# First attention of a two-layer network: the scores below the 32nd pushed down before the exponential, by ScalarE and GpSimd, instead of a masked product on VectorE

## The chip, the cores and the metric

One core of one Trainium2 chip runs the whole network as one program. The metric is the device time of an execution in microseconds. The engines are TensorE (PE), VectorE (DVE), ScalarE (ACT), GpSimd (POOL) and SyncE (SP); each takes its instructions in order, and they wait for one another by semaphores.

## The reference, cut to what matters

The network has four parts on x of 16 batches by 256 rows by 128: a first cross-attention with a convolution and a feed-forward part, a small mixture of experts, a second cross-attention over all 1601 context rows, and a second mixture. Only the scores of the first are concerned. Each of its 4 heads has 256 query rows a batch and 1601 keys:

```
scores = einsum('bthd,bghd->bhtg', Q, K) / sqrt(DH)
topv, topi = top_k(scores, 32)
probs = softmax(topv)
attn = zeros_like(scores).at[..., topi].set(probs)
attn_mean = attn.mean(axis=1)          # over the heads
c_t = einsum('btg,bgd->btd', attn_mean, V)
```

So of a row's 1601 scores the 32 largest go through a softmax, all others become zero, and the four heads are averaged.

## The kernel before, in words

`attention0_phase` (from L417) works in **slots**. A slot is 128 query rows of one head of one batch: 2 tiles of rows by 4 heads make 8 slots (NS) a batch, 128 slots in all. `j` is the slot's number over all batches, `s` that within its batch. Batch 0 and batch 15 are written out, the 14 between run in a loop of two batches each (`walk`, L516). The order of the work is written out by hand: every engine has a `step(b, ...)` that goes over s from 0 to 7, and what it does beside the slot hangs on s. A slot goes like this:

- TensorE, `scores_of` (L682): the slot's scores, 128 x 1601, into four banks of PSUM; there is one such buffer. It is issued two slots ahead.
- ScalarE, `scores_out_of` (L813): copies them to `sc` in SBUF (four buffers), also two slots ahead.
- VectorE, `pieces_of` (L934): the eight largest of each of 32 pieces of 51 scores, one slot ahead. These 32 small maxima are put two at a time between the links of the next chain, so that its latencies are covered (`link`, inside `step`).
- VectorE: four times the eight largest of the 256 candidates (L966), each followed by a replacement of those found (L972). After the first, `negm` (minus the row's maximum, L968) is given to ScalarE. The last value is the 32nd largest, unless a piece held more than eight of the 32. Three reductions and a comparison (L974 to L978) tell whether that may be so, a **doubt**: the largest candidate left, or the eighth of any piece, is not under the threshold.
- ScalarE, `exp_of` (L820): exp of all 1601 scores into `pr` (one buffer for each s).
- VectorE, L986: the masked product. `pr` is multiplied by (score >= threshold).
- TensorE, `count_doubts` (L723): adds the doubts of the 128 rows by a product with a column of ones, into one number in PSUM. It is the first thing of TensorE's step.
- VectorE, `settle` (L924): converts the number of the slot before to an integer in SBUF (L927), loads it into a register and branches. If it is over zero, `select_all` (L912) finds the 32 largest again from all 1601 scores: four long maxima (L917), four replacements (L918) and a product (L919). Then it gives `top_ready` and `pr_ready`. That stands just before the masked product.
- ScalarE, `denominator` (L826): exp of the 32 values with their sum. VectorE, `weight` (L903): its reciprocal, times the row mask / 4. GpSimd, `make_diag` (L578): a diagonal matrix of it.
- TensorE, `transpose_probs` (L693): for the four heads of a tile, pr times the diagonal, added up in PSUM: that transposes, scales and averages at once. 13 key blocks go in four groups through two PSUM tiles (`tps`). GROUPS says which groups fall at which s: {1: (0,), 2: (1, 2), 3: (3,)}; the same at s + 4 for the other tile. Then `times_ctx` (L711) multiplies with the context.

Beside the slots, TensorE and ScalarE prepare the next batch and the later parts through one PSUM tile `misc`: a product, then ScalarE's copy, then the next product. There are 17 such jobs a batch: the film product (s = 0 and 4; `film`, L718 and L850), queries (s = 0), keys (s = 1, 2), transposed context (s = 4, 5), values (s = 6, 7). ScalarE's copies of them stand behind the slot's exponential and scores copy in its queue. GpSimd splits the keys into three bf16 parts (`split_keys`, L598, all at s = 3: three casts, two subtractions of 1601 columns), applies the film (L588), and SyncE stores the parts.

The next stage is `conv_phase` (from L996).

## Time and profile before

| | us |
|---|---|
| median of 3 runs (4032.58 to 4047.92) | 4040.31 |
| the profiled execution | 4040.28 |
| its span | 4038.7 |

| engine | busy us | share of the span |
|---|---|---|
| TensorE, products | 2940.5 | 73% |
| TensorE, weight loads | 1659.7 | 41% |
| VectorE | 2832.6 | 70% |
| ScalarE | 1684.6 | 42% |
| GpSimd | 550.0 | 14% |

A time in the span is in microseconds from its start. The first attention lies from about 193 to about 1846 us. A row of the profile names the engine, the line of the code, the operation, what is written and read, and how often; after a bar the busy time, the mean of one in ns, and the idle time of the engine just before it with what ended it. Matmuls overlap, so their durations add up to a little more than the time they take. PEclk is the granted TensorE clock as a share of 2.4 GHz.

### The profile page before, as it was taken

The numbers are of one execution on the slowest core, as the hardware profiler recorded it, in microseconds if no ns is written. First come the engines' busy times: TensorE is split into PE (matmuls) and PEld (weight loads), VectorE is DVE, ScalarE is ACT, GpSimd is POOL, SyncE is SP. The second block draws the span as 40 slices with busy tenths as digits, with TensorE's granted clock in tenths as the row PEclk, the third lists the DMA queues.
The fourth block names the chain that finished last, engine by engine and source line by source line (L and its number), as shares of the span: only waits on it lengthen the run. The fifth ranks groups of instructions, "written<-read, shape, count | busy, mean of one in ns | idle before, by whom it ended". The sixth has DMA issues, their size and how long they took to land. (4 is left out here: it accounts for less than half of the span.)

```text
span 4038.7 us, 71774 instructions
## 1 busy us (share of the span) xinstructions
PE 2940.5 (73%) x21156; PEld 1659.7 (41%) x21156; DVE 2832.6 (70%) x9302; ACT 1684.6 (42%) x2879; POOL 550.0 (14%) x721
## 2 busy tenths in 40 slices
PE   0047876878867787878965552489899899899748
PEld 0025554545544555657943220033333333333335
DVE  5578878888888887880055564988888888888212
ACT  1124433434433444431011001077777777778612
POOL 1011221212211222220011001200000000000133
PEclk9868888888888888886577665589999999999869
DMA  1000100100000010002301000522222222222121
GB/s 44 17 8 29 36 30 24 35 24 34 31 24 26 34 35 30 30 24 95 125 3 52 0 0 31 83 46 58 63 55 58 62 56 58 62 55 41 44 67 49
DMA packets 134711, 169.79 MB, mean 42 GB/s; under 512 B 50962, under 2 KB 103887, under 8 KB 134331
## 3 DMA queue, kind: packets, MB, share of 16 engines
q1 hardware_dynamic: 129694, 154.76, 13.9%
q0 software_dynamic: 4640, 10.76, 0.8%
q8 instruction: 144, 2.36, 0.2%
q14 instruction: 233, 1.91, 0.2%
HBM read 112.39 MB, written 53.51 MB: 41 GB/s over the span
## 5 line engine op out<-in xcount | busy, mean ns | idle before, releaser
L1919 DVE TENSOR_REDUCE mx<-wps 128x2 f32<-128x802 f32 x1024 | 957.9, 989 | 153.2 <-PE wps L1812 136.6
L1893 ACT ACTIVATE pb<-sps 128x512 f32<-128x512 f32 (+1 forms) x1664 | 896.6, 596 | 375.0 <-PE sps L1837 361.2
L937 DVE MAX8 cand<-sc 128x8 f32<-128x51 f32 (+1 forms) x4096 | 587.8, 198 | 34.8 <-ACT sc L818 34.6
L1850 PE MATMUL ops<-pb,va 128*32 128x256 f32 x6656 | 554.0, 406 | 7.6 <-ACT ot L1899 7.1
L690 PE MATMUL scores<-ctxT,qT 97*128 97x512 f32 (+1 forms) x1024 | 482.5, 624 | 6.3 <-ACT sc L818 3.2
L1812 PE MATMUL wps<-ks,qs 56*128 56x401 bf16 x2048 | 384.8, 361 | 109.0 <-DVE mx L1919 57.6
L706 PE MATMUL tps<-diag,pr 128*128 128x128 f32 (+1 forms) x3328 | 418.6, 288 | 5.7 <-issue 5.5
L1837 PE MATMUL sps<-qs,ks 59*128 59x256 bf16 (+1 forms) x3328 | 364.6, 284 | 63.6 <-DMA qs<-guards 63.1
L706 PEld LDWEIGHTS tps<-diag,pr 128*128 128x128 f32 (+1 forms) x3328 | 404.3, 200 | 8.3 <-issue 7.9
L986 DVE SCALAR_TENSOR_TENSOR pr<-sc,top,pr 128x1601 f32<-128x1601 f32 x128 | 251.4, 1964 | 151.4 <-issue 147.3
L690 PEld LDWEIGHTS scores<-ctxT,qT 97*128 97x128 f32 x1024 | 221.4, 228 | 254.7 <-issue 245.4
L824 ACT ACTIVATE pr<-sc,negm 128x1601 f32<-128x1601 f32 x128 | 208.5, 1629 | 225.9 <-DVEq L969 225.4
L1837 PEld LDWEIGHTS sps<-qs,ks 59*128 59x128 bf16 (+1 forms) x3328 | 120.7, 96 | 404.7 <-ACT pb L1893 242.5
L586 POOL TENSOR_SCALAR diag<-ident,rden 128x128 f32<-128x128 f32 x128 | 90.3, 705 | 1141.2 <-DVEq L910 937.1
L818 ACT COPY sc<-scores 128x1601 f32<-128x1601 f32 x128 | 190.5, 1488 | 79.8 <-PE scores L690 79.5
L1850 PEld LDWEIGHTS ops<-pb,va 128*32 128x32 f32 x6656 | 133.4, 110 | 213.1 <-issue 107.1
L1812 PEld LDWEIGHTS wps<-ks,qs 56*128 56x128 bf16 x2048 | 110.9, 97 | 244.4 <-DVE mx L1919 170.5
L1724 POOL COPY va<-vn 128x128 f32<-128x128 f32 (+1 forms) x208 | 50.3, 294 | 1095.8 <-PE ops L1850 1017.4
L840 ACT COPY prT<-tps 128x512 f32<-128x512 f32 (+1 forms) x128 | 64.6, 505 | 256.6 <-PE tps L706 256.6
L966 DVE MAX8 top<-cleft 128x8 f32<-128x256 f32 x384 | 157.2, 409 | 0.1
L972 DVE MATCH_REPLACE8 cleft<-top,cleft 128x256 f32<-128x256 f32 x384 | 157.1, 409 | 0.0
L728 PE MATMUL dps<-onecol,doubt 128*1 128x1 f32 x256 | 24.2, 163 | 175.4 <-DVEq L932 174.3
(370 smaller groups left out, 3610.4 us busy)
## 6 DMA issues: line engine op xcount, KB each, us to landing
ks<-keys SPq DMA_DIRECT2D x896, 50.0 KB
keys<-kpart SPq DMA_DIRECT2D x48, 400.2 KB, 2.8
toep<-kernpad SPq DMA_DIRECT2D x8, 2048.0 KB, 8.1
qs<-queries SPq DMA_DIRECT2D x896, 8.0 KB
values<-vs SPq DMA_DIRECT2D x16, 832.0 KB, 3.4
vn<-values SPq DMA_DIRECT2D x16, 832.0 KB, 4.8
ctxn<-in_ctx_dram SPq DMA_DIRECT2D x16, 576.0 KB
sorted<-m_blank SPq DMA_DIRECT2D x39, 130.0 KB, 3.2
```

The source lines that it names most:

```text
L690: ins = t.matmul(scores[:, c:c + n], q, ctxT[par][0:C + 1, c:c + n], start=True, stop=True)
L706: ins = t.matmul(tps[g % 2][0:kn(kt), (kt % 4) * P:(kt % 4) * P + P], pr[s0 + h][:, kt * P:kt * P + kn(kt)], diag[s0 + h][:, :], start=(h ...
L818: s_.copy(sc[s % 4][:, :], scores[:, 0:NK]).then_inc(scores_out, 1)
L824: s_.activation(pr[s][:, :], sc[s % 4][:, :], ACT.Exp, bias=negm[:, s:s + 1]).then_inc(exp_done, 1)
L937: st.add(v.max(cand[s % 2][:, n, :], sc[s % 4][:, c:c + w]))
L966: link(v.max(tp[:, 8 * r:8 * r + 8], x))
L986: st.link(v.scalar_tensor_tensor(out=pr[s][:, :], in0=sc[s % 4][:, :], scalar=tp[:, TOPK - 1:TOPK], in1=pr[s][:, :], op0=ALU.is_ge, op1=AL ...
L1812: ins = t.matmul(buf[:, 512 * odd:512 * odd + WIN], qs[par][r, h + odd, q * P:q * P + P], ks[par][r, h // 2, (WIN - 1) * c:(WIN - 1) * c + ...
L1837: ins = t.matmul(sps[(UNITS * g + u) % SB][0:kn(kt), i, :], ks[par][r, h // 2, kt * P:kt * P + kn(kt)], qs[par][r, h, :], start=True, stop ...
L1850: ins = t.matmul(ops[VW * i:VW * i + VW, 0:S], va[par][0:kn(kt), kt, 4 * g + i, :], pb[(UNITS * g + 2 * kt + i % 2) % 8][0:kn(kt), i // 2, :],
L1893: nc.scalar.activation(pb[(UNITS * g + u) % 8][0:rows_, :, :], sps[(UNITS * g + u) % SB][0:rows_, :, :], ACT.Exp).then_inc(p_ready, 1)
L1919: v.tensor_reduce(mx4[:, q, h:h + 2, c], both, AX.X, ALU.max).then_inc(work_read, 1)
```

## The change

The masked product goes. Instead, scores below the threshold are pushed far down before the exponential, so that it gives zero for them:

- GpSimd, `cut_of(s)`: waits for the threshold (`thr_ready`), clips it to +-2^46, multiplies it by 2^80 (`cutoff`), and makes `negm`. Three operations on one column.
- ScalarE, `below_of(s)`, one step later: relu(2^80 * (threshold - score)) into `pr`: zero for kept scores, huge for the others.
- GpSimd, `keep_of(s)`, in that same later step: `pr` = score - `pr`, over 128 x 1601.
- ScalarE, `exp_of(s)`, two steps later: exp of `pr` in place. It waits for `settled` and `kept_ready`.

The doubts are found by counting: one comparison over the 256 candidates and one over the 32 eighths, each with its sum, give for a row the candidates not under the threshold plus the pieces whose eighth is not; the branch asks whether the sum over the rows exceeds 128 x 32. ScalarE (`doubts_of`) copies the number from PSUM to SBUF as an integer, where VectorE did. VectorE's last replacement goes, `negm` and the product with the row mask go to GpSimd. `settle` and `weight` stand at the end of VectorE's slot. `select_all` now makes `pr` itself: a copy, eight long operations, a comparison and a sum. The transposes move one slot later (GROUPS), `split_keys` is spread over s = 3 to 7, the masks' constant is 2^45 in place of 1e30, and GpSimd clears this stage's semaphores at the end of its part of `conv_phase`.

```diff
 BIG = 1e30
+HIDDEN = 2.0 ** 45
 GONE = -3e38
...
             st.link(v.tensor_copy(mf[:, :], m8[:, :]))
-            v.tensor_scalar(mf[:, :], mf[:, :], BIG, -BIG, ALU.mult, ALU.add).then_inc(mask_done, 1)
+            v.tensor_scalar(mf[:, :], mf[:, :], HIDDEN, -HIDDEN, ALU.mult, ALU.add).then_inc(mask_done, 1)
...
+        k.used = []
+
         def sem(name):
-            return ctx.enter_context(nc.semaphore(name))
+            k.used.append(ctx.enter_context(nc.semaphore(name)))
+            return k.used[-1]
...
         cleft = sb("cleft", [P, len(PIECES), 8])
-        rest = sb("rest", [P, 2])
+        count = sb("count", [P, 2])
         doubt = sb("doubt", [P, 2])
-        doubts = sb("doubts", [1, 1], mybir.dt.int32)
+        doubts = sb("doubts", [1, 2], I32)
+        cut, cutoff = sb("cut", [P, NS]), sb("cutoff", [P, NS])
         onecol = sb("onecol", [P, 1])
...
         misc_ready, misc_out = sem("misc_ready"), sem("misc_out")
-        negm_ready, exp_done, top_ready, den_done, pr_ready = (sem("negm_ready"), sem("exp_done"), sem("top_ready"),
-                                                               sem("den_done"), sem("pr_ready"))
+        thr_ready, cut_ready, below_ready, kept_ready = sem("thr_ready"), sem("cut_ready"), sem("below_ready"), sem("kept_ready")
+        settled, exp_done, den_done = sem("settled"), sem("exp_done"), sem("den_done")
         rden_ready, diag_ready = sem("rden_ready"), sem("diag_ready")
...
                                                            sem("kparts_saved"), sem("vs_saved"))
-        doubt_ready, doubts_ready, general_step = sem("doubt_ready"), sem("doubts_ready"), sem("general_step")
+        doubt_ready, doubts_ready, doubts_out, general_step = (sem("doubt_ready"), sem("doubts_ready"), sem("doubts_out"),
+                                                               sem("general_step"))
         slot_begun, pool_passed = sem("slot_begun"), sem("pool_passed")
...
         HALVES = ((0, 1), (2, 3))
-        GROUPS = {1: (0,), 2: (1, 2), 3: (3,)}
+        GROUPS = {2: (0, 1), 3: (2, 3)}
+
+
+        STEEP, LIMIT = 2.0 ** 80, 2.0 ** 46
...
                 pool.sem_inc(pool_passed, 1)
+                st.link(g.tensor_tensor(rden[:, s:s + 1], rden[:, s:s + 1], k.tmask[:, bass.ds(QT * b + s // H0, 1)],
+                                        ALU.mult))
                 g.tensor_scalar(diag[s][:, :], ident[:, :], rden[:, s:s + 1], None, ALU.mult).then_inc(diag_ready, 1)
+
+            def cut_of(s, j):
+
+                pool.wait_ge(thr_ready, j + 1)
+                pool.sem_inc(pool_passed, 1)
+                c = cut[:, s:s + 1]
+                st.link(g.tensor_scalar(c, top[:, s % 4, TOPK - 1:TOPK], LIMIT, -LIMIT, ALU.min, ALU.max))
+                st.add(g.tensor_scalar(cutoff[:, s:s + 1], c, STEEP, 0.0, ALU.mult, ALU.add))
+                st.link(g.tensor_scalar(negm[:, s:s + 1], top[:, s % 4, 0:1], -1.0, 0.0, ALU.mult, ALU.add))
+                pool.sem_inc(cut_ready, 1)
+
+            def keep_of(s, j):
+
+                pool.wait_ge(below_ready, j + 1)
+                g.tensor_tensor(pr[s][:, :], sc[s % 4][:, :], pr[s][:, :], ALU.subtract).then_inc(kept_ready, 1)
...
-            def split_keys(b):
-
-                pool.wait_ge(misc_out, prep_jobs(b, "k")[1])
-                for n in range(3):
+            def split_keys(b, s):
+
+                if s == 3:
+                    pool.wait_ge(misc_out, prep_jobs(b, "k")[1])
+                n = (s - 3) // 2
+                if s % 2:
                     if n or not first_batch(b):
...
                     pool.sem_inc(kparts_ready, 1)
-                    if n < 2:
-                        st.link(g.tensor_tensor(kf[:, :], kf[:, :], kpart[:, :], ALU.subtract))
+                else:
+                    st.link(g.tensor_tensor(kf[:, :], kf[:, :], kpart[:, :], ALU.subtract))
...
                         copy_x(b + 1, 1 - par)
+                    j = NS * b + s
+                    if not (first and s == 0):
+                        keep_of((s - 1) % NS, j - 1)
+                    cut_of(s, j)
                     if not (first and s < 2):
...
                         film(QT * (b - 1), film_job(0, b))
-                    if s == 3:
-                        split_keys(b)
+                    if s >= 3:
+                        split_keys(b, s)
                     if s == 4 and not first:
...
             walk(pool, step)
+            keep_of(NS - 1, NS * B - 1)
             for s in (NS - 2, NS - 1):
...
                 if groups[0] == 0:
-                    pe.wait_ge(pr_ready, jobs)
+                    pe.wait_ge(exp_done, jobs)
                     pe.wait_ge(diag_ready, jobs)
...
                 if not isinstance(j, int) or j > 0:
-                    pe.wait_ge(pr_ready, j)
+                    pe.wait_ge(doubts_out, j)
                 t.matmul(dps[0:1, 0:1], doubt[:, s % 2:s % 2 + 1], onecol[:, :], start=True, stop=True).then_inc(doubts_ready, 1)
...
                 if not isinstance(j, int) or j >= 4:
-                    act.wait_ge(pr_ready, j - 3)
+                    act.wait_ge(settled, j - 3)
+                    act.wait_ge(kept_ready, j - 3)
                 s_.copy(sc[s % 4][:, :], scores[:, 0:NK]).then_inc(scores_out, 1)
...
-            def exp_of(b, s, j, first):
-                act.wait_ge(negm_ready, j + 1)
-                if not first:
-                    act.wait_ge(tps_ready, TPG * (QT * (b - 1) + s // H0 + 1))
-                s_.activation(pr[s][:, :], sc[s % 4][:, :], ACT.Exp, bias=negm[:, s:s + 1]).then_inc(exp_done, 1)
+            def below_of(s, j):
+
+                act.wait_ge(cut_ready, j + 1)
+                s_.activation(pr[s][:, :], sc[s % 4][:, :], ACT.Relu, bias=cutoff[:, s:s + 1], scale=-STEEP
+                              ).then_inc(below_ready, 1)
+
+            def exp_of(s, j):
+                act.wait_ge(kept_ready, j + 1)
+                act.wait_ge(settled, j + 1)
+                s_.activation(pr[s][:, :], pr[s][:, :], ACT.Exp, bias=negm[:, s:s + 1]).then_inc(exp_done, 1)
+
+            def doubts_of(s, j):
+                act.wait_ge(doubts_ready, j + 1)
+                s_.copy(doubts[0:1, s % 2:s % 2 + 1], dps[0:1, 0:1]).then_inc(doubts_out, 1)
...
-                act.wait_ge(top_ready, j + 1)
+                act.wait_ge(settled, j + 1)
                 s_.activation(etop[:, s % 2, :], top[:, s % 4, :], ACT.Exp, bias=negm[:, s:s + 1],
...
                         denominator((s - 2) % NS, j - 2)
-                    exp_of(b, s, j, first)
+                    if not (first and s == 0):
+                        doubts_of((s - 1) % NS, j - 1)
+                        below_of((s - 1) % NS, j - 1)
+                    if not (first and s < 2):
+                        exp_of((s - 2) % NS, j - 2)
                     if not (last and s >= NS - 2):
...
             walk(act, step)
+            doubts_of(NS - 1, NS * B - 1)
+            below_of(NS - 1, NS * B - 1)
             for s in (NS - 2, NS - 1):
                 denominator(s, NS * (B - 1) + s)
+                exp_of(s, NS * (B - 1) + s)
             for n in range(QT):
...
-            def weight(b, s, j):
-
+            def weight(s, j):
...
                 dve.wait_ge(den_done, j + 1)
-                st.link(v.reciprocal(rden[:, s:s + 1], den[:, s:s + 1]))
-                st.link(v.tensor_tensor(rden[:, s:s + 1], rden[:, s:s + 1],
-                                        k.tmask[:, bass.ds(QT * b + s // H0, 1)], ALU.mult))
-                dve.sem_inc(rden_ready, 1)
-
-            def select_all(s):
+                v.reciprocal(rden[:, s:s + 1], den[:, s:s + 1]).then_inc(rden_ready, 1)
+
+            def select_all(s, j):
...
                 every = Steps(dve, general_step)
-                x, tp = sc[s % 4][:, :], top[:, s % 4, :]
+                x, tp, kept = sc[s % 4][:, :], top[:, s % 4, :], pr[s][:, :]
+                dve.wait_ge(kept_ready, j + 1)
+                every.link(v.tensor_copy(kept, x))
                 for r in range(TOPK // 8):
...
                     every.link(v.match_replace(x, tp[:, 8 * r:8 * r + 8], x, GONE))
-                every.link(v.scalar_tensor_tensor(out=pr[s][:, :], in0=x, scalar=-2e38, in1=pr[s][:, :],
-                                                  op0=ALU.is_le, op1=ALU.mult))
+                every.link(v.tensor_scalar(x, x, -2e38, -BIG, ALU.is_gt, ALU.mult))
+                every.link(v.tensor_tensor(kept, kept, x, ALU.add))
                 every.restart()
...
-                dve.wait_ge(doubts_ready, j + 1)
+                dve.wait_ge(doubts_out, j + 1)
                 dve.sem_inc(slot_begun, 1)
-                st.link(v.tensor_copy(doubts[:, :], dps[0:1, 0:1]))
-                n = dve.value_load(doubts[0:1, 0:1], min_val=0, max_val=P)
-                with dve.If(n > 0):
-                    select_all(s)
-                dve.sem_inc(top_ready, 1)
-                dve.sem_inc(pr_ready, 1)
+                n = dve.value_load(doubts[0:1, s % 2:s % 2 + 1], min_val=0, max_val=P * len(PIECES) * 9)
+                with dve.If(n > P * TOPK):
+                    select_all(s, j)
+                dve.sem_inc(settled, 1)
...
                     x, y = (t[:, :, :].rearrange("p n e -> p (n e)") for t in (cand[s % 2], cleft))
+                    done = st.n
+                    for _ in range(2):
+                        next(ahead, None)
+                    if done:
+                        dve.wait_ge(dve_step, done)
                     for r in range(TOPK // 8):
                         link(v.max(tp[:, 8 * r:8 * r + 8], x))
-                        if r == 0:
-                            link(v.tensor_scalar(negm[:, s:s + 1], tp[:, 0:1], -1.0, None, ALU.mult))
-                            dve.sem_inc(negm_ready, 1)
-                            if not (first and s < 2):
-                                weight(b if s >= 2 else b - 1, (s - 2) % NS, j - 2)
-                        link(v.match_replace(y, tp[:, 8 * r:8 * r + 8], x, GONE))
-                        x = y
-                    st.add(v.tensor_reduce(rest[:, 0:1], cand[s % 2][:, :, 7], AX.X, ALU.max))
-                    link(v.tensor_reduce(rest[:, 1:2], y, AX.X, ALU.max))
-                    d = doubt[:, s % 2:s % 2 + 1]
-                    link(v.tensor_reduce(d, rest[:, :], AX.X, ALU.max))
-                    link(v.tensor_scalar(d, d, tp[:, TOPK - 1:TOPK], None, ALU.is_ge))
+                        if r < TOPK // 8 - 1:
+                            link(v.match_replace(y, tp[:, 8 * r:8 * r + 8], x, GONE))
+                            x = y
+                    dve.sem_inc(thr_ready, 1)
+
+                    c, x = count[:, s % 2:s % 2 + 1], cand[s % 2][:, :, :].rearrange("p n e -> p (n e)")
+                    link(v.tensor_scalar(y, x, tp[:, TOPK - 1:TOPK], 0.0, ALU.is_ge, ALU.add, accum_out=c))
+                    link(v.tensor_scalar(y[:, 0:len(PIECES)], cand[s % 2][:, :, 7], tp[:, TOPK - 1:TOPK], c, ALU.is_ge,
+                                         ALU.add, accum_out=doubt[:, s % 2:s % 2 + 1]))
                     dve.sem_inc(doubt_ready, 1)
...
                         pass
+                    if not (first and s < 2):
+                        weight((s - 2) % NS, j - 2)
                     if not (first and s == 0):
                         settle((s - 1) % NS, j - 1)
-                    dve.wait_ge(exp_done, j + 1)
-                    dve.sem_inc(slot_begun, 1)
-                    st.link(v.scalar_tensor_tensor(out=pr[s][:, :], in0=sc[s % 4][:, :], scalar=tp[:, TOPK - 1:TOPK],
-                                                   in1=pr[s][:, :], op0=ALU.is_ge, op1=ALU.mult))
                 st.restart()
...
             for s in (NS - 2, NS - 1):
-                weight(B - 1, s, NS * (B - 1) + s)
+                weight(s, NS * (B - 1) + s)
...
             walk(pool, step)
+            for used in k.used:
+                pool.sem_clear(used)
...
         def _(pe):
```

## Rows read from the trace of the kernel before

**Rows 1.** Busy time by stretch: the stage's steady part, and two stretches of 3 us in it

```profile
core 0: us, PE busy (x) PEld busy (x) DVE busy (x) ACT busy (x) POOL busy (x), PEclk, DMA share, GB/s
320.00:1785.00 1465.00, 1139.39 (x5969) 785.76 (x5967) 1211.16 (x6356) 599.29 (x876) 304.47 (x297) 0.86 0.09 30
...
1413.00:1416.00 3.00, 1.68 (x4) 0.95 (x5) 1.82 (x4) 0.69 (x3) 2.61 (x3) 0.50 0.34 131
...
1431.00:1434.00 3.00, 3.00 (x29) 3.00 (x29) 3.00 (x19) 0.96 (x2) 0.00 (x0) 1.00 0.00 0
```

**Rows 2.** page, part 5: the costly groups of this stage

```profile
L937 DVE MAX8 cand<-sc 128x8 f32<-128x51 f32 (+1 forms) x4096 | 587.8, 198 | 34.8 <-ACT sc L818 34.6
...
L986 DVE SCALAR_TENSOR_TENSOR pr<-sc,top,pr 128x1601 f32<-128x1601 f32 x128 | 251.4, 1964 | 151.4 <-issue 147.3
...
L824 ACT ACTIVATE pr<-sc,negm 128x1601 f32<-128x1601 f32 x128 | 208.5, 1629 | 225.9 <-DVEq L969 225.4
...
L818 ACT COPY sc<-scores 128x1601 f32<-128x1601 f32 x128 | 190.5, 1488 | 79.8 <-PE scores L690 79.5
```

**Rows 3.** timeline of VectorE, one slot (start, us, engine line, what, idle before)

```profile
1053.51 0.43 DVE L966 MAX8 top<-cand 128x8 f32<-128x256 f32 x1 [0.23 <-DVE pr L986]
...
1059.13 0.41 DVE L975 TENSOR_REDUCE rest<-cleft 128x1 f32<-128x256 f32 x1
...
1061.21 0.13 DVE L927 CAST doubts<-dps 1x1 int32<-1x1 f32 x1
...
1062.49 1.89 DVE L986 SCALAR_TENSOR_TENSOR pr<-sc,top,pr 128x1601 f32<-128x1601 f32 x1 [1.16 <-issue]
...
1064.61 0.43 DVE L966 MAX8 top<-cand 128x8 f32<-128x256 f32 x1 [0.23 <-DVE pr L986]
```

**Rows 4.** who waited for whom, 1307.2 to 1495.1 us (total, times, longest)

```profile
PE dps L728 <- DVEq L932: 7.4, 5, 2.1
...
PE misc L658 <- ACT fs L855: 8.1, 2, 6.0
...
ACT pr L824 <- DVEq L969: 27.9, 13, 5.7
```

**Rows 5.** timeline of TensorE, over two batches

```profile
1307.10 0.19 PE L728 MATMUL dps<-onecol,doubt 128*1 128x1 f32 x2 [0.88 <-DVEq L932]
...
1354.55 0.19 PE L728 MATMUL dps<-onecol,doubt 128*1 128x1 f32 x2
...
1364.60 0.69 PE L658 MATMUL misc<-ident,xn 128*128 128x128 f32 x2 [6.01 <-ACT fs L855]
...
1461.27 5.81 PE L690 MATMUL scores<-ctxT,qT 97*128 97x512 f32 x8
...
1473.92 3.01 PE L690 MATMUL scores<-ctxT,qT 97*128 97x512 f32 x8
...
1476.77 7.36 PE L706 MATMUL tps<-diag,pr 128*128 128x128 f32 x64
...
1494.96 0.19 PE L728 MATMUL dps<-onecol,doubt 128*1 128x1 f32 x2 [0.88 <-DVEq L932]
```

**Rows 6.** GpSimd's groups by shape, 193 to 1830 us

```profile
L608 POOL TENSOR_TENSOR kf<-kf,kpart 128x1601 f32<-128x1601 f32 x32 | 103.3, 3227 | 6.2 <-POOL kpart L605 6.2
...
L593 POOL TENSOR_TENSOR XF<-XF,fs 128x128 f32 x28 | 12.7, 455 | 2.2
```

**Rows 7.** the general path's first line, all its instructions

```profile
L917 DVE MAX8 top<-sc x24: 1828/1828/1830, 241.5 to 1266.7; 128x8 f32<-128x1601 f32 x24
```

**Rows 8.** timeline of TensorE, ends of the middle batches

```profile
346.06 0.19 PE L728 MATMUL dps<-onecol,doubt 128*1 128x1 f32 x2
...
1729.90 0.19 PE L728 MATMUL dps<-onecol,doubt 128*1 128x1 f32 x2
...
1822.07 0.19 PE L728 MATMUL dps<-onecol,doubt 128*1 128x1 f32 x2
```

**Rows 9.** ScalarE's small operations

```profile
L829 ACT ACTIVATE etop<-top,negm x128: 308/321/325, 258.7 to 1823.4; 128x32 f32<-128x32 f32 x128
```

## The prediction

> **What bounds the kernel now.** Start with the busy time of the stage's steady part: TensorE is busy 1139 of 1465 us and VectorE 1211, ScalarE 599, GpSimd 304 [rows 1]. So two engines stand close together, and a share of busy time can't say which one sets the pace. The costly groups name the work on VectorE: 4096 small maxima, and one masked product of 1.96 us in each of 128 slots, which this change removes [rows 2]. The timeline of VectorE then gives the slot: from one first maximum (1053.51) to the next (1064.61) are 11.10 us, without a stall except around the branch, 1.28 us from the conversion's start to the product's, and 0.23 behind the product [rows 3]. Eight such slots are 88.8 us a batch.
>
> Then TensorE. I call what it does from one doubt count (L728) to the next a step; eight make a batch. Sixteen steps, from 1307.10 to 1494.96, take 187.86 us, so a batch is 93.9 us [rows 5], 5.1 more than VectorE's eight slots: now and then VectorE waits too. Of the 187.86, TensorE waits 7.4 for VectorE's doubts, of which the first 0.88 belong to the step before [rows 4, 5]: 6.5 us. It also waits 8.1 us in two waits for ScalarE's copy of the film product, 6.01 the one and so 2.1 the other [rows 4, 5]. ScalarE is late there because its exponential waits for VectorE's row maximum (27.9 us in 13 waits) [rows 4]; the excess of the long wait, 3.9 us, is VectorE's too. Without these TensorE would need 187.86 - 6.5 - 3.9 = 177.4, **88.7 us a batch**. The bound is VectorE, but TensorE with its waits for ScalarE comes 5 us behind it. That is the number on which this prediction turns.
>
> **The change, part by part.**
>
> VectorE loses the product with the gap behind it (1062.49 to 1064.61, 2.12 us), the conversion (0.13), the negation of the maximum, the mask product of the weight, the last replace and two of four reductions. In their place come two comparisons that also count. Neither their form nor their count shows in the trace: from the reduction over 256 candidates (0.41 [rows 3]) I take 0.5 and 0.3; from below nothing, from above 1 us each. What the small removed ones save beyond what the counts cost I put at 0.8 us, twice that same 0.41 (bounds: a loss of 1, a gain of 1.6). Result: 11.1 - 2.1 - 0.8 = some 8.2 us a slot, 66 us a batch, bounds 59 and 80. The branch stays, and its 1.2 us is in the 8.2. Even the upper bound is under 88.7, so VectorE stops being the bound, and its exact price no longer matters.
>
> ScalarE gains the steep rectifier over 1601 scores, which I cost as the exponential of the same size, 1.63, and the copy of one count, 0.3 by its small operation [rows 2, 9] (nothing to 0.5). 128 x 1.9 = 243 us over the stage: from 599 of 1465 us (41%) to some 56%. Ahead of the copy of the next scores its queue in a step is 0.3 + 0.3 + 1.63 + 1.63, then 1.49 for the copy [rows 2, 9]: 5.4 us, where before it was 3.4 and a wait for the maximum. The film copy then lands about 6 us into a step, as in the better step of today. That hides nothing new but costs nothing either.
>
> GpSimd gains the subtraction, 3.23 us by the one row of that size, although its second input there is bf16 (3.2 to 4.2 if two full inputs cost more), and four operations on one column, each under the 0.46 of a 128-wide one [rows 6]; I take 0.2 each, 0.8 together, bounds 0.3 and 1.8. That is 4.0 us a slot on top of 304 us in the some 127 slots of the steady part's 1465 us, 2.4: **6.4 us a step**, against a step of 11.3. The key split is spread over slots 3 to 7, so that at most one pass of it falls into a step. The worst step (4, with the subtraction of the split and a film) ends about 2 us into the next one, which has room. Behind the subtraction in its queue wait the cut-off of the next slot and the diagonal that TensorE needs two slots later: both have half a step to spare. The new dependence (threshold, cut-off, rectifier, subtraction, exponential) is 0.6 + 1.63 + 3.23 + 1.63 = 7.1 us, laid over two steps of 11, so it is latency and no pace, except at the end of the last batch, where it adds some 5 us before the last transposes.
>
> The Trainium skill, in GPSIMD Engine Reference, section "Engine selection", advises VectorE for elementwise work, because a two-input operation is about twice slower on GpSimd. The rows agree on the ratio, 3.23 to 1.96 [rows 2, 6]. If that ratio set the time the change would lose; it is a rival below.
>
> TensorE does the same products. But its transposes leave steps 1 and 5 for steps 2 and 6, and 3 and 7: a group moves one step later. What was behind long transposes (the evacuation of the scores) is now exposed in steps 1 and 5, about 1 us a batch. The clock matters more. After waits it is at 0.50, the lower level, and in dense transposes at 1.00 [rows 1]; the same scores take 5.81 or 3.01 us [rows 5]. Today each batch has two half-speed stretches, around steps 5 and 1. I expect two still, starting in steps 4 and 0, and reaching a little into steps 6 and 2. For all this I take +1.6 us a batch: 88.7 + 1.6 = **90.3**. Bounds: -6 (both stretches of scores at full clock, 2 x 2.8), and +10 (below).
>
> **The sum.** Between the first step of batch 1 and that of batch 15 are 1383.8 us [rows 8] = 14 x 93.9 + 69 for four passes of the general path, 17.3 each; there are six in all, as 24 long maxima in fours show [rows 7].
> Middle batches: 14 x (93.9 - 90.3) = 50 us less.
> General path: it gets longer by a copy, a comparison and a sum against one product, 9 x 1.83 = 16.5 [rows 7] before, about 19.5 after (bounds 18.5 and 20.2: two more passes of 1 to 1.83). But VectorE's slot now begins with the scores' copy, 5.5 us into a step, and ends 8.2 later, 2.4 into the next of 11.3; ScalarE asks for its result at the start of the one after, some 8 us later. So 11.5 remain of it: 4 x (17.3 - 11.5) = 23 less.
> First batch: VectorE bounds the first four steps, which have no transposes. Four slots at 3 us are 12, the two general passes there 4 more: 16 less (bounds 5 and 30).
> Last batch: 92.2 us (1729.90 to 1822.07 [rows 8]) without preparations for a next one; TensorE needs about 77: 15 less, minus the 5 of the tail.
> The clearing of some 38 semaphores by GpSimd in the next stage: 2 us, nothing to 5.
> Together 50 + 23 + 16 + 10 - 2 = 97 us less. The profiled execution took 4040.28, the median of the runs is 4040.31, so both give **3943 us**, 2.4% less.
>
> **The rivals.**
> A, the forecast: TensorE and ScalarE in turn set 87 to 94 us a batch: 3897 to 3995. Chance 0.60.
> B, the clock holds: with VectorE's waits gone both slow stretches shorten, a batch is 84, the sum 88 less than mine: 3855. For it: TensorE is denser. Against it: the waits for ScalarE in steps 0 and 4 stay. 0.14.
> C, VectorE was the only bound: 128 x 2.9 = 371 us less, 3670. For it the row of the product; against it TensorE's own 88.7. 0.03.
> D, no change: a batch of 96 to 98.5, because GpSimd's late subtraction holds ScalarE's exponential and behind it the copy of the scores, 6 to 8 us a batch: 4020 to 4060. It needs GpSimd over 9 us a step, and the rows give 6.4. 0.12.
> E, slower by the clock: steps 0, 1, 4 and 5 lose the transposes that kept TensorE dense, so it stays at the lower level until well into steps 2 and 6: scores (2 x 2.8) and transposes (7.36 for 64 [rows 5], so about 4 more for half of them) at half speed, 10 us a batch more, 100: 4083. It decides from where a batch passes 97.3, 93.9 plus the other gains (47) over 14. For it: after a wait of 2 us the whole of the next scores runs slow today, 5.81 us [rows 5]. Against: today it comes back inside the same dense step. 0.08. The Trainium skill, in TensorE: Matmul & The Clock Gate, section "HAM oscillation — how this bites in real kernels", says that idle gaps between bursts put the clock back to half; that rule speaks against this change, and the trace agrees with it as far as 0.50 in [rows 1] shows.
> F, slower by the ratio of the engines: each slot pays 1.63 + 3.23 - 1.96 = 2.9 us more, 128 x 2.9 = 371: 4410. It needs the five links to be walked within one slot; the order written out gives them three. 0.03.
>
> **How the numbers follow.** About 0.5%, 20 us, is what a measurement of this kernel can tell from no change. Faster: A, B and C, 0.77. Same: D, 0.12. Slower: E and F, 0.11. The range 3830 to 4035 takes in A, B and the nearer part of D (0.07), and leaves out C, the rest of D, E and F, together 0.19.
>
> **What would show it.** Right: no product; about 8.2 us of VectorE work a slot with idle before its small maxima, released by ScalarE's scores copy; TensorE's waits for VectorE (L728) near nothing in clean batches; a batch of 90 us; the waits for the film copy at 2 to 2.6 us each. Wrong: batches of 84 or less with a mean clock over 0.9 (B), scores at 5.81 in steps 2 and 6 (E), or ScalarE's exponential waiting for the subtraction (D, F).

## The result, and the profile of the changed kernel

| | before | after |
|---|---|---|
| median, us | 4044.11 (4032.58 to 4048.04, 4 runs) | 3936.51 (3922.91 to 3957.01, 4 runs) |
| ratio, 95% interval | | 0.9743 [0.9692, 0.9794] |
| profiled execution's span, us | 4038.7 | 3955.4 |

The change makes the program 2.6% faster. Forecast were 3943 us, 3830 to 4035. The profiled execution of the changed kernel, 3957.01 us, is the slowest of its four, so the two traces differ by 83.3 us and the medians by 107.6.

Part 5 of the page for the changed kernel (mean in ns behind the comma, then idle time ahead and what ended it), against [rows 2]:

```profile
L983 DVE MAX8 cand<-sc 128x8 f32<-128x51 f32 (+1 forms) x4096 | 575.2, 198 | 432.3 <-ACT sc L852 423.2
L612 POOL TENSOR_TENSOR pr<-sc,pr 128x1601 f32<-128x1601 f32 x128 | 458.7, 3583 | 548.5 <-ACT pr L857 544.9
...
L723 PE MATMUL scores<-ctxT,qT 97*128 97x512 f32 (+1 forms) x1024 | 519.9, 664 | 9.7 <-ACT sc L852 5.2
...
L857 ACT ACTIVATE pr<-sc,cutoff 128x1601 f32<-128x1601 f32 x128 | 208.3, 1627 | 24.3 <-POOLq L607 24.3
L863 ACT ACTIVATE pr<-pr,negm 128x1601 f32<-128x1601 f32 x128 | 206.8, 1615 | 1.6 <-POOL pr L612 1.6
```

The masked product is gone. VectorE's small maxima take what they took, but now stand 423 us idle until ScalarE has copied the scores (34.6 before): VectorE is no longer the bound. The exponential waits 1.6 us in all for the subtraction.

Busy time by stretch: the steady part, a clean batch (one without a general pass: batch 12, from its first count, L761, to that of the next), two short stretches inside it, and batch 14, clean as well:

```profile
core 0: us, PE busy (x) PEld busy (x) DVE busy (x) ACT busy (x) POOL busy (x), PEclk, DMA share, GB/s
326.00:1650.00 1324.00, 1120.84 (x5699) 755.75 (x5697) 863.24 (x5371) 732.81 (x1057) 754.64 (x847) 0.84 0.09 32
...
1383.67:1476.04 92.37, 82.01 (x402) 53.61 (x402) 55.92 (x376) 52.17 (x76) 53.23 (x60) 0.82 0.09 33
1395.00:1405.00 10.00, 9.22 (x14) 3.44 (x12) 3.51 (x25) 6.14 (x8) 4.86 (x6) 0.50 0.00 0
1411.00:1420.00 9.00, 8.26 (x69) 7.43 (x67) 6.87 (x46) 3.36 (x4) 2.01 (x6) 1.00 0.00 0
...
1563.20:1649.90 86.70, 76.00 (x402) 51.62 (x401) 55.81 (x376) 51.85 (x75) 52.86 (x59) 0.88 0.10 35
```

TensorE fills 85% of the steady part (78% in [rows 1]) and VectorE 65% (83%). In a clean batch VectorE has 55.92 us of work, 7.0 a step. The two clean batches hold the same 402 products and differ by 5.7 us, with the granted clock at 0.82 and 0.88. The timeline of TensorE through the slower one shows where:

```profile
1383.67 0.19 PE L761 MATMUL dps<-onecol,doubt 128*1 128x1 f32 x2
1383.79 3.01 PE L723 MATMUL scores<-ctxT,qT 97*128 97x512 f32 x8
...
1389.42 0.43 PE L691 MATMUL misc<-ident,xn 128*128 128x128 f32 x2 [1.71 <-ACT fs L898]
...
1394.99 5.81 PE L723 MATMUL scores<-ctxT,qT 97*128 97x512 f32 x8
...
1405.51 5.68 PE L723 MATMUL scores<-ctxT,qT 97*128 97x512 f32 x8
1411.03 7.36 PE L739 MATMUL tps<-diag,pr 128*128 128x128 f32 x64
...
1437.06 0.64 PE L682 MATMUL misc<-ident,ctxn 128*96 128x128 f32 x4 [1.63 <-ACT fs L898]
...
1448.11 4.87 PE L723 MATMUL scores<-ctxT,qT 97*128 97x512 f32 x8 [0.26 <-ACT ctxT L815]
```

It waits 1.7 and 1.6 us for the film copy and never for VectorE's doubts, but scores at the lower level (5.7 against 3.01 us) now reach into step 2, and 4.87 into step 6. In step 2 that is so in four of the ten clean batches; in the other six the step takes 12.33 us, as before. In step 6 it is so in all ten (15.0 to 16.5 us against 13.1 to 13.3). The same view at the ends of the middle batches and at the tail:

```profile
337.81 0.19 PE L761 MATMUL dps<-onecol,doubt 128*1 128x1 f32 x2
...
1649.91 0.19 PE L761 MATMUL dps<-onecol,doubt 128*1 128x1 f32 x2
...
1728.87 0.19 PE L761 MATMUL dps<-onecol,doubt 128*1 128x1 f32 x2
...
1736.28 14.57 PE L739 MATMUL tps<-diag,pr 128*128 128x128 f32 x104 [5.80 <-ACT pr L863]
```

The middle batches take 1312.1 us against 1383.8 [rows 8]. The ten clean ones average 89.4 (94.2 before), the four with a general pass 104.6 (110.4).

### The profile page after: what moved, and what is told of

Same layout as the page of the kernel before. It is cut to its first block and busy times, and to the rows that moved or that the text cites. A ratio compares the mean times of both kernels' runs of the same rounds, so it can differ in the third digit from the quotient of the medians.

```text
span 3955.4 us, 71843 instructions
## 1 busy us (share of the span) xinstructions
PE 2982.3 (75%) x21156; PEld 1668.2 (42%) x21156; DVE 2503.7 (63%) x8546; ACT 1869.1 (47%) x3135; POOL 1078.5 (27%) x1361
## 5 line engine op out<-in xcount | busy, mean ns | idle before, releaser
L983 DVE MAX8 cand<-sc 128x8 f32<-128x51 f32 (+1 forms) x4096 | 575.2, 198 | 432.3 <-ACT sc L852 423.2
L612 POOL TENSOR_TENSOR pr<-sc,pr 128x1601 f32<-128x1601 f32 x128 | 458.7, 3583 | 548.5 <-ACT pr L857 544.9
L723 PE MATMUL scores<-ctxT,qT 97*128 97x512 f32 (+1 forms) x1024 | 519.9, 664 | 9.7 <-ACT sc L852 5.2
L739 PE MATMUL tps<-diag,pr 128*128 128x128 f32 (+1 forms) x3328 | 401.0, 283 | 14.5 <-POOL diag L597 7.5
L739 PEld LDWEIGHTS tps<-diag,pr 128*128 128x128 f32 (+1 forms) x3328 | 391.0, 195 | 15.7 <-issue 9.1
L723 PEld LDWEIGHTS scores<-ctxT,qT 97*128 97x128 f32 x1024 | 236.0, 242 | 281.2 <-issue 269.8
L857 ACT ACTIVATE pr<-sc,cutoff 128x1601 f32<-128x1601 f32 x128 | 208.3, 1627 | 24.3 <-POOLq L607 24.3
L863 ACT ACTIVATE pr<-pr,negm 128x1601 f32<-128x1601 f32 x128 | 206.8, 1615 | 1.6 <-POOL pr L612 1.6
L1416 DVE SCALAR_TENSOR_TENSOR m_xg<-m_ep,m_wt,m_xg 128x128 f32<-128x128 f32 x256 | 89.8, 351 | 56.0 <-PE m_ep L1444 40.2
```

The costliest lines, as they stand in the source:

```text
L612: g.tensor_tensor(pr[s][:, :], sc[s % 4][:, :], pr[s][:, :], ALU.subtract).then_inc(kept_ready, 1)
L723: ins = t.matmul(scores[:, c:c + n], q, ctxT[par][0:C + 1, c:c + n], start=True, stop=True)
L739: ins = t.matmul(tps[g % 2][0:kn(kt), (kt % 4) * P:(kt % 4) * P + P], pr[s0 + h][:, kt * P:kt * P + kn(kt)], diag[s0 + h][:, :], start=(h ...
L857: s_.activation(pr[s][:, :], sc[s % 4][:, :], ACT.Relu, bias=cutoff[:, s:s + 1], scale=-STEEP).then_inc(below_ready, 1)
L863: s_.activation(pr[s][:, :], pr[s][:, :], ACT.Exp, bias=negm[:, s:s + 1]).then_inc(exp_done, 1)
L983: st.add(v.max(cand[s % 2][:, n, :], sc[s % 4][:, c:c + w]))
```

## The experiments

Twelve runs in three series, each series beside its own runs of the kernel before, so the ratios are what compares. The changed kernel ran again in the second series:

> The kernel after itself, again, as the mark for the others on this chip: 0.97 to 0.98 of before.

| kernel | median us | ratio to before | middle batches, us |
|---|---|---|---|
| before | 4044.11 | 1 | 1383.8 |
| changed | 3936.51 | 0.9743 [0.9692, 0.9794] | 1312.1 |
| changed, again | 3927.75 | 0.9735 [0.9689, 0.978] | 1295.0 |
| before, product cut | 3967.48 | 0.9843 [0.9818, 0.9868] | 1322.7 |
| before, GROUPS of after | 4105.98 | 1.0181 [1.0161, 1.0201] | 1440.7 |
| changed, GROUPS of before | 4090.38 | 1.0137 [1.0102, 1.0173] | 1434.8 |
| the same, ScalarE reordered | 4084.57 | 1.0122 [1.0085, 1.0158] | 1433.1 |
| changed, one more reduction on VectorE a slot | 3955.54 | 0.9812 [0.9795, 0.9828] | 1301.6 |
| changed, two more | 4092.99 | 1.0153 [1.0136, 1.017] | 1415.6 |
| changed, waits of TensorE filled | 3940.89 | 0.9763 [0.9721, 0.9805] | 1310.8 |
| changed, ScalarE reordered | 3927.55 | 0.9731 [0.9682, 0.978] | 1290.4 |
| both | 3929.23 | 0.9745 [0.97, 0.979] | 1291.1 |
| changed, relu cut | 3880.76 | 0.9615 [0.9578, 0.9651] | 1256.0 |
| changed, subtraction cut | 3907.48 | 0.9689 [0.9654, 0.9724] | 1284.9 |

The last column is of the one profiled execution each, from batch 1's step 0 to batch 15's. Two executions of the changed kernel differ there by 17 us: their clean batches average 89.4 and 88.3 us, those with a general pass 104.6 and 103.1. So a trace of another kernel is held against both.

### The product alone

```diff
-                    st.link(v.scalar_tensor_tensor(out=pr[s][:, :], in0=sc[s % 4][:, :], scalar=tp[:, TOPK - 1:TOPK],
-                                                   in1=pr[s][:, :], op0=ALU.is_ge, op1=ALU.mult))
+                    st.link(v.scalar_tensor_tensor(out=pr[s][:, 0:2], in0=sc[s % 4][:, 0:2], scalar=tp[:, TOPK - 1:TOPK],
+                                                   in1=pr[s][:, 0:2], op0=ALU.is_ge, op1=ALU.mult))
```

> The kernel before, with VectorE's masked product done over 2 of 1601 columns: the selection is left out, and nothing is given to ScalarE or GpSimd in its place. Theory (TensorE, with its waits for ScalarE, stands 5 us a batch behind VectorE): the slot of VectorE falls to 9.2 us, the batch only to 88 to 91, so the time falls by 60 to 110 us, to 3935 to 3985, much like the change. Rival (VectorE alone sets the pace): 128 x 1.9 = 243 us less, 3800. Rival (the product was hidden): 4030 to 4050.

Measured: 0.9843, about 62 us less. Of the 1.9 us a slot, 243 in all, a quarter comes back, at the weak end of what was expected. Its timeline of TensorE has what holds the rest, in batch 13:

```profile
1527.62 0.19 PE L728 MATMUL dps<-onecol,doubt 128*1 128x1 f32 x2 [0.88 <-DVEq L932]
1537.12 0.19 PE L728 MATMUL dps<-onecol,doubt 128*1 128x1 f32 x2 [2.34 <-DVEq L932]
```

TensorE still waits for VectorE in two steps of the eight, as long as before: over the middle batches 108.7 us against 109.5. What came back is mostly the wait for ScalarE's copy of the film product, 44.9 us in all against 88.4, since the exponential ahead of that copy no longer waits so long for VectorE's maximum. A clean batch takes 90.0 us (94.2 before). The changed kernel's ratio is a further 0.010 lower; which of its other parts on VectorE (the count in place of the last replacement, the conversion moved to ScalarE) gives that was not tried one by one.

### The order of the transposes, in the kernel before

```diff
-        GROUPS = {1: (0,), 2: (1, 2), 3: (3,)}
+        GROUPS = {2: (0, 1), 3: (2, 3)}
```

> The kernel before, with only the transposes one slot later, as in the change. Theory: VectorE sets the pace at 93.9 us a batch and TensorE has the room, so within 15 us of before, and in the profile steps 1 and 5 are lighter. Rival (the clock: without dense transposes in steps 1 and 5 TensorE stays at the lower level into steps 2 and 6): 3 to 6 us a batch more, 40 to 90 us slower, 4085 to 4135.

Measured: 1.0181, 77 us more (4105.98 against 4029.11 in this series). My theory fell, and the rival's range was met; its reason, the clock, is only a part of it. Steps 4 and 5 of a clean batch average 22.3 us together, which is VectorE's two slots (22.2), so they give up only 1.6 us (23.9 before) of the 3.7 that a group takes, and steps 0 and 1 give up 4.4. Steps 2, 3, 6 and 7 grow by 10.1 together. On top stand scores at the lower level in the dense steps, here step 2 of batch 12, behind a light step that ended in a wait:

```profile
1512.29 4.94 PE L690 MATMUL scores<-ctxT,qT 97*128 97x512 f32 x8
...
1522.52 0.19 PE L728 MATMUL dps<-onecol,doubt 128*1 128x1 f32 x2 [2.00 <-DVEq L932]
1522.64 4.71 PE L690 MATMUL scores<-ctxT,qT 97*128 97x512 f32 x8
1527.19 7.36 PE L706 MATMUL tps<-diag,pr 128*128 128x128 f32 x64
```

Step 2 is 12.33 us at full clock (the changed kernel has the same step) and here 14.03 at the least, so the clock costs at least 1.7 us a batch there. So in a kernel that VectorE bounds, this order costs. How the 77 us divide between imbalance and clock, no run separates.

### The same order undone, in the changed kernel

```diff
-        GROUPS = {2: (0, 1), 3: (2, 3)}
+        GROUPS = {1: (0,), 2: (1, 2), 3: (3,)}
```

> The changed kernel with one part undone: the transposes are issued in steps 1, 2, 3 and 5, 6, 7 as in the kernel before (groups 0 | 1, 2 | 3), not in 2, 3 and 6, 7. Worked out from the trace of the changed kernel: the diagonal comes from GpSimd about 8.1 us after the count that opens a step, so steps 1 and 5 grow from 8.6 and 8.3 to about 12 to 12.5 (8.1 of waiting, 3.7 of transposes, little behind), while steps 3 and 7 shrink from 11.0 and 13.1 to the 8.8 and 9.9 of the kernel before. Theory 1 (the low clock of steps 2 and 6 is brought on by the light steps 1 and 5 ahead of them): with work back in steps 1 and 5 the scores of steps 2 and 6 run at full clock again, their batches stay near 12.3 and 13.3 for these two steps, a batch comes to about 87.7 us, and the time to 3895 to 3935. Theory 2 (the low level sets in once per so much work wherever it stands, as the run with filler products suggested): nothing comes back, the wait for the diagonal is added, batches of 91 to 94 us, and 3955 to 4000 us.

Measured: 1.0137, that is 4.1% above the changed kernel (1.0137/0.9735). Both theories fell. The timeline of TensorE in steps 1 and 5 of batch 12:

```profile
1492.66 0.19 PE L761 MATMUL dps<-onecol,doubt 128*1 128x1 f32 x2
1492.78 5.81 PE L723 MATMUL scores<-ctxT,qT 97*128 97x512 f32 x8
1500.91 6.20 PE L739 MATMUL tps<-diag,pr 128*128 128x128 f32 x32 [2.32 <-issue]
...
1509.81 0.19 PE L761 MATMUL dps<-onecol,doubt 128*1 128x1 f32 x2
...
1538.77 5.32 PE L723 MATMUL scores<-ctxT,qT 97*128 97x512 f32 x8
1549.58 5.78 PE L739 MATMUL tps<-diag,pr 128*128 128x128 f32 x32 [5.49 <-issue]
```

and of GpSimd in step 5:

```profile
1538.21 3.23 POOL L636 TENSOR_TENSOR kf<-kf,kpart 128x1601 f32<-128x1601 f32 x1
...
1544.03 3.57 POOL L612 TENSOR_TENSOR pr<-sc,pr 128x1601 f32<-128x1601 f32 x1
...
1548.78 0.60 POOL L597 TENSOR_SCALAR diag<-ident,rden 128x128 f32<-128x128 f32 x1
```

I had costed the wait right in step 1 (the diagonal is ready 8.1 us after the count) but not in step 5, where the subtraction of the key split and the film stand ahead of it and it is ready 10.7 us after the count (1538.65). In both steps the transposes start 0.2 us after the diagonal is ready. And I had taken them at 3.7 us: they take 3.68 at full clock (7.36 for 64), but behind these waits they take 6.20 and 5.78, at a mean clock of 0.60 and 0.65. Steps 1 and 5 are 17.2 and 18.1 us instead of 12 to 12.5, and the clean batch near 99. With the subtraction in GpSimd's queue the late order is what makes the change pay.

> As the run before it (transposes back in steps 1, 2, 3 and 5, 6, 7), and besides ScalarE's exponential of steps 0 and 4 put behind the copies that TensorE waits for. By theory 1 what this saves in steps 0 and 4 (1.1 and 0.5 us, as its own run showed) is now kept, since a fuller step 1 or 5 follows: 10 to 25 us under the run with the transposes moved alone. By theory 2 it is given back as it was: within 8 us of that run.

Its edit is the one above with the reordering of ScalarE described below. Measured: 1.0122, 6 us less, which is less than the two intervals can tell apart. The light steps 0 and 4 became 0.9 and 0.6 us shorter and the steps behind them together as much longer: those wait for the diagonal.

### How far is VectorE from being the bound?

One more reduction over the 1601 scores in each slot, and in the second kernel two (`range(2)`):

```diff
+                    for _ in range(1):
+                        st.link(v.tensor_reduce(spare[:, :], sc[s % 4][:, :], AX.X, ALU.max))
                     if not (first and s < 2):
                         weight((s - 2) % NS, j - 2)
```

> The kernel after, with one more reduction over 1601 columns on VectorE in every slot, about 1.85 us, its result unused. Theory (VectorE has some 25 us to spare in a batch): 8 x 10 = 80 us of VectorE a batch against 90, so within 15 us of after, 3920 to 3955. Rival (VectorE still sets the pace, or its slot stands in the chain that does): 128 x 1.85 = 237 us more, 4175; half of that would be 4055.

> The kernel after, with two such reductions, 3.7 us a slot. Theory: VectorE's slot is 11.8 us, 94 to 95 a batch, over TensorE's 90, and it sets the pace again as before the change: 96 to 100 us a batch, 80 to 150 us more than after, 4015 to 4085. Rival (VectorE sets the pace in all of them): 128 x 3.7 = 474 us more, 4410. Rival (VectorE doesn't matter at all here): 3940.

A reduction took 1.80 to 1.82 us, so one a slot is 231 us in all and two are 466. Measured: 0.9812 and 1.0153. The first 231 us of extra work cost 0.8%, about 30 us, twice the 15 that I had allowed. The profiled execution shows some 6 us of it, in the first batch (it ends at 343.82 against 337.81 and 337.01); its middle batches are between those of the changed kernel's two executions. The second reduction cost 3.4%, some 137 us. Busy time over the middle batches, one reduction and two:

```profile
343.82:1645.43 1301.61, 1087.56 (x5615) 739.61 (x5614) 1058.88 (x5460) 726.63 (x1050) 749.69 (x839) 0.86 0.09 33
```

```profile
356.68:1772.30 1415.62, 1113.33 (x5616) 752.08 (x5616) 1257.85 (x5542) 727.66 (x1050) 749.46 (x839) 0.84 0.09 30
```

VectorE's work of a slot is 1058.88/112 = 9.5 us in the one and 11.2 in the other, the general passes counted in. In a clean batch of the second it is 10.6 (84.59 us in batch 14), and the branch comes on top; the kernel before had 11.1 with its gaps. So in the middle batches VectorE had between 1.8 and 3.6 us a slot to spare. The second came out 8 us above the 4015 to 4085 that I gave.

### The clock: filling TensorE's waits

```diff
+            def fill(n):
...
+                pe.wait_ge(doubts_out, seen[0])
+                for _ in range(n):
+                    t.matmul(dps[:, P:2 * P], ident[:, :], ident[:, :], start=True, stop=True)
...
                 t.matmul(misc[:, :], uT[:, :], k.WVF[:, :], start=True, stop=True).then_inc(misc_ready, 1)
+                fill(7)
```

with two more products ahead of each preparation that waits for the copy before it.

> The kernel after, with products of the identity with itself put into TensorE's waits for ScalarE: seven behind the film product in steps 0 and 4, two before each later product of a preparation for queries, keys and context (steps 0, 1, 4, 5); their results are unused. Theory (the waits of steps 0 and 4 bring the clock to the lower level, and that costs the scores of steps 5, 6, 1 and often 2 some 2.8 us each): the granted clock of the middle batches goes from 0.84 to over 0.95, a batch from 90 to 81 to 84, 85 to 125 us less than after. Rival (the level has another cause, or the fillers take what they give): clock as in after, and within 30 us of it, above rather than below.

Measured: 0.9763, no gain. The expectation fell. The fillers did raise the clock, and they did shorten the light steps. Busy time of this kernel's middle part, and its timeline of TensorE from step 0 of batch 14:

```profile
350.00:1600.00 1250.00, 1067.24 (x6012) 781.34 (x6012) 814.37 (x5043) 687.90 (x995) 707.83 (x793) 0.90 0.09 32
```

```profile
1567.81 1.73 PE L678 MATMUL dps<-ident 128*128 128x128 f32 x14
...
1573.37 0.19 PE L778 MATMUL dps<-onecol,doubt 128*1 128x1 f32 x2
1573.49 3.01 PE L739 MATMUL scores<-ctxT,qT 97*128 97x512 f32 x8
...
1580.52 0.19 PE L778 MATMUL dps<-onecol,doubt 128*1 128x1 f32 x2
1580.64 4.71 PE L739 MATMUL scores<-ctxT,qT 97*128 97x512 f32 x8
```

0.90 against 0.84 in the same window of the changed kernel, the scores of step 1 at 3.01 and the step 7.15 us. But the lower level then comes in step 2 (14.0 to 17.0 us in 11 of the 14 middle batches, 12.33 in the others; in the changed kernel's two traces it was 7 and 4 of the 14), in step 6 (14.6 to 18.0), and at times in step 7 (up to 16.9) or 0 (up to 14.1), which are 13.2 and 11.5 at the most in the changed kernel's clean batches. Why the level moves there the run does not show.

### ScalarE: order and load

First the order: in steps 0 and 4 the exponential goes behind the copies that TensorE waits for.

```diff
-                    if not (first and s < 2):
+                    behind = s in (0, 4) and not last
+                    if not (first and s < 2) and not behind:
                         exp_of((s - 2) % NS, j - 2)
```

(it is issued inside the preparations of these steps instead).

> The kernel after, with ScalarE's exponential of steps 0 and 4 moved behind the scores' copy, the film copy and the first preparation copy. Theory (in the light steps 0 and 4 ScalarE's queue sets the pace: 0.5 + 0.1 + 1.6 + 1.6 + 1.5 us before the film copy): the film copy comes some 1.2 us earlier in both, TensorE's wait of 1.7 before the next product falls to about 0.5, 0.5 to 1.2 us off each of the two steps, 15 to 35 us less than after. Rival (the exponential is needed where it stands, or VectorE or GpSimd is behind it): no change, or a wait of the transposes for it.

> Both, the order and the fillers. Theory: with the waits shorter by the order, the seven fillers stick out by up to 1 us in each of steps 0 and 4, so no more than a_warm alone, 80 to 130 us less than after. Rival (fillers take what they give): like a_order or above it.

Measured: 0.9731 and 0.9745 against the 0.9735 of the changed kernel in the same series. For both kernels the gain that I expected did not come. In the reordered one the film waits fall to 1.2 us, steps 0 and 4 to about 10.1 and to 7.1 to 7.5 us, and nothing that can be measured comes of it (four runs of 3919 to 3943 us beside 3921 to 3940; a gain of 10 us could hide in that): step 6 stays at 15.0 to 16.6, and step 2 at 14.3 to 17.1 in seven of the fourteen batches (seven and four in the changed kernel's two traces).

Then the load:

```diff
-                s_.activation(pr[s][:, :], sc[s % 4][:, :], ACT.Relu, bias=cutoff[:, s:s + 1], scale=-STEEP
+                s_.activation(pr[s][:, 0:2], sc[s % 4][:, 0:2], ACT.Relu, bias=cutoff[:, s:s + 1], scale=-STEEP
...
-                g.tensor_tensor(pr[s][:, :], sc[s % 4][:, :], pr[s][:, :], ALU.subtract).then_inc(kept_ready, 1)
+                g.tensor_tensor(pr[s][:, :], sc[s % 4][:, :], sc[s % 4][:, :], ALU.subtract).then_inc(kept_ready, 1)
```

> The changed kernel with ScalarE's relu over 2 of 1601 columns; the subtraction takes the scores from themselves, so that the selection is left out. ScalarE loses 1.55 us a step (about 198 us in all) and the chain to the exponential gets 1.6 us shorter. My theory (TensorE's own work and its clock set the time; ScalarE's part is cover): within 15 us of the changed kernel, its ratio to the kernel before 0.970 to 0.978; the waits of TensorE for the copy of the FiLM products shrink from 1.6 us to under 1, and the time comes back as slow scores in steps 2 and 6. Rival (what ScalarE took on delays the copies that TensorE needs, and that costs time): at least 14 times 1.6 us faster, 3905 us or less, ratio under 0.968.

Measured: 0.9615, 47 us under the changed kernel. My theory fell, and the rival's number was met. But this run shortens more than ScalarE's work. The subtraction now reads `sc` as both of its inputs, and that took 2.86 us where it was 3.58:

```profile
L612 POOL TENSOR_TENSOR pr<-sc 128x1601 f32<-128x1601 f32 x128 | 365.7, 2857 | 546.1 <-ACT pr L857 542.5
```

So the chain to the exponential is 2.1 us shorter, of which the relu gives only 1.3, and this run alone can't tell GpSimd's part from ScalarE's. The traces say where the time came back: the ten clean batches average 85.6 us (89.4 and 88.3 in the changed kernel's two traces), the four with a general pass 99.9 (104.6 and 103.1), the last batch 72.6 (79.0 and 79.5). The last two, 20 to 25 us together, come back in the next experiment too, where ScalarE keeps its load. The other 26 to 37 us, in the clean batches, do not come back there though GpSimd loses all of the subtraction: these are ScalarE's. The shorter waits are only a part of these: two waits for the film copy, 0.5 us shorter each, are 14 us over fourteen batches. The busy time of its batches 13 and 14:

```profile
1421.00:1512.00 91.00, 81.30 (x404) 53.60 (x404) 55.83 (x376) 41.94 (x76) 47.45 (x60) 0.83 0.09 33
1512.00:1591.00 79.00, 68.57 (x399) 48.41 (x397) 55.93 (x376) 41.63 (x75) 47.04 (x59) 0.98 0.11 38
```

and the timeline of TensorE in the second of them, steps 4 to 6:

```profile
1557.34 0.64 PE L682 MATMUL misc<-ident,ctxn 128*96 128x128 f32 x4 [1.18 <-ACT fs L898]
...
1559.34 3.01 PE L723 MATMUL scores<-ctxT,qT 97*128 97x512 f32 x8
...
1565.05 3.01 PE L723 MATMUL scores<-ctxT,qT 97*128 97x512 f32 x8 [0.26 <-ACT ctxT L815]
1568.40 7.41 PE L739 MATMUL tps<-diag,pr 128*128 128x128 f32 x64 [0.34 <-issue]
```

The same work takes 90.85 us at a mean clock of 0.83 and 79.58 at 0.98, and TensorE's waits for ScalarE agree within 0.5 us each: **between these two batches the clock is worth 11 us**. Three of the fourteen batches are near 80 us here (9, 12 and 14); in the reordered kernel, with film waits as short, none is under 84. What tips it was not found.

### GpSimd: the load of the subtraction

```diff
-        STEEP, LIMIT = 2.0 ** 80, 2.0 ** 46
+        STEEP, LIMIT = 2.0 ** -20, 2.0 ** 46
...
-                g.tensor_tensor(pr[s][:, :], sc[s % 4][:, :], pr[s][:, :], ALU.subtract).then_inc(kept_ready, 1)
+                g.tensor_tensor(pr[s][:, 0:2], sc[s % 4][:, 0:2], pr[s][:, 0:2], ALU.subtract).then_inc(kept_ready, 1)
```

> The changed kernel with GpSimd's subtraction over 2 of 1601 columns and a small steepness, so that the relu's result stays finite; the selection is left out. GpSimd loses 3.5 us a step (450 us in all), and the chain to the exponential gets as much shorter. My theory: GpSimd has time to spare, within 15 us of the changed kernel (ratio 0.970 to 0.978). Rival D (GpSimd's late result holds up the exponential, the diagonal and so the transposes, or its reads hold up VectorE's pieces): 25 us faster or more, ratio under 0.968. If VectorE's reductions get shorter beside an idle GpSimd while the time stays, they only lengthen VectorE's waits.

Measured: 0.9689, 20 to 29 us under the changed kernel, just short of the rival's 0.968 and past my theory's bound; the intervals of the two ratios overlap, but all four runs (3904.58 to 3913.43) are under all eight of the changed kernel (from 3920.83). The clean batches hardly change: 88.5 us on average against 89.4 and 88.3, and the small maxima keep their 198 ns, so GpSimd's reads hold up nothing on VectorE. The gain is in the batches with a general pass, 99.9 against 104.6 and 103.1, and in the last one, 71.9 against 79.0 and 79.5. All instructions of the general path's first line, in the changed kernel

```profile
L963 DVE COPY pr<-sc x6: 976/995/996, 242.5 to 1197.1; 128x1601 f32<-128x1601 f32 x6
...
  POOL pr L612: 20.6, 5
```

and without the subtraction:

```profile
L963 DVE COPY pr<-sc x6: 974/987/1004, 239.5 to 1179.1; 128x1601 f32<-128x1601 f32 x6
...
  POOL pr L612: 3.9, 3
```

`select_all` begins by waiting for the subtraction of its slot (`kept_ready`), because it writes the same `pr`. That wait is 4.1 us on average, five times of six, on VectorE with everything behind it. The time lands at TensorE as a wait for ScalarE's copy of the keys. Of who waited for whom in batch 4, the changed kernel and then the one without the subtraction (total, times, longest):

```profile
PE misc L704 <- ACT kf L833: 14.9, 2, 14.1
```

```profile
PE misc L704 <- ACT kf L833: 11.5, 2, 10.8
```

## Why the forecast held, step by step

- **VectorE is the bound, TensorE with its waits 5 us behind.** Right in what it forecasts: that only the part down to TensorE's 88.7 comes back is shown by the product alone (62 of 243 us, a clean batch of 90.0) and from the other side by the extra reductions (231 us more cost 30, the next 235 cost 137). As a picture it is too simple. In the trace of before VectorE is the bound in some steps only: TensorE waits for its doubts in steps 4 and 5 of a clean batch, and through ScalarE's film copy in steps 0 and 4, while steps 2 and 3 take TensorE's own 12.33 and 8.83 us in most batches.
- **VectorE's slot, 8.2 us.** Right to within 1: its busy time is 55.92/8 = 7.0 us a step and the branch comes on top; with 1.8 more it was still no bound in the middle batches, with 3.6 it was. The counts take 0.48 and 0.31 us, with 0.08 each to read the sum; 0.5 and 0.3 were forecast.
- **ScalarE costs nothing.** Here the step failed. The copy of the count is 0.13 us instead of 0.3 and the film copy comes as early as said (waits of 1.7, not 2 to 2.6), but "hides nothing new but costs nothing either" does not hold: with the relu cut, and the subtraction 0.7 us shorter by that edit, 47 us came back. Of these the 26 to 37 in the clean batches are ScalarE's, part of it shorter waits, part of it clock; the rest, in the general passes and the last batch, comes as well from a shorter subtraction. (The sum for its busy share gives 57%, not 56; 732.81/1324 = 55% was measured.)
- **GpSimd, 6.4 us a step.** 53.23/8 = 6.7, 0.3 over: the subtraction is 3.58 us, not 3.23 (inside its bounds), and the other new operations are as small as said. "Both have half a step to spare" holds only because the transposes moved: a group earlier, the diagonal is 2.3 to 5.5 us late, and the change is a loss of 1.4%.
- **TensorE, +1.6 a batch.** 89.4 in the clean batches against 90.3. The mechanism was right: slow stretches start in steps 0 and 4 and reach into step 6 always, by most of its scores (1.9 us in batch 12), and into step 2 in four of ten (two of ten in the second trace), there by nearly all of them (2.7). Rival E named this; it priced the transposes at half speed too, and mostly they are not: 7.36 us for 64 in batch 12. In batch 9 the level reaches them as well (9.28 us, a step 2 of 17.0).
- **Middle batches and general path.** 71.7 us less, 73 forecast, but differently made up: batches gave 4.8 each, not 3.6 (67 us for 50), and the general passes 4, not 23: one still costs 15.2 us (104.6 - 89.4), where 11.5 were forecast and 16.2 were paid before (110.4 - 94.2). The missed term is VectorE's own wait for the subtraction, 4.1 us; the pass's operations themselves take 18.8 us, 19.5 were forecast. The run without the subtraction has 11.4 (99.9 - 88.5). That the total came out within 2 us is luck: 17 us too little for the batches and 19 too much for the general passes cancel.
- **First batch** -8.3 (346.06 to 337.81), not -16, and why was not followed up; **last batch** 79.0 from 92.2, -13.2 for -15; **tail** from the last count to the last copy +5.0 for +5; all that comes after +4.9 for +2, which is less than one kernel's executions differ by: from the last count to the end of the program are 2226.5 us in this trace and 2213.7 in the other trace of the changed kernel (2216.6 before).
- The sum of these is 83 us in the traces for 97 forecast; the medians say 108. The run-to-run spread of one kernel is that large (the middle batches were 1312.1 and 1295.0 us in two executions).
- **B, the clock holds,** needed batches of 84 on average. It did not happen (86.6 is the shortest in the first trace, 85.7 in the second), nor with fillers (clock 0.90, single batches of 84); with the relu cut two of the last four middle batches were under 80. So the gain exists, and shorter waits alone don't bring it. **F and C** are excluded by the result. Of **D** this is left: the subtraction comes late in the general passes, for VectorE, and in the last batch.

The rule of the Trainium skill, GPSIMD Engine Reference, section "Engine selection", is borne out as a ratio: 3.58 us on GpSimd and 1.83 on VectorE (L968, the same shape with two full inputs). It did not decide, since GpSimd had the time: it was 14% busy before and is 27% after, and 57% in this stage (754.64/1324). The Trainium skill's TensorE: Matmul & The Clock Gate, section "HAM oscillation — how this bites in real kernels", blames idle gaps for the half clock. The trace agrees that the lower level follows the waits; that filling them brings time back was not seen here: the clock rose from 0.84 to 0.90 and the time stayed.
